# Inverse norms of q and k from Ln and Exp in place of Sqrt and a reciprocal

## The chip, the core and the metric

The kernel runs on one core of a Trainium2 chip. The metric is the time of one execution on the device in microseconds (us), as the median of three runs. TensorE does the matmuls and transposes, VectorE and ScalarE work element by element, GpSimd takes part of the element work, and SyncE issues the transfers. The engines run side by side, each through its own list of instructions in order, and wait for each other by semaphores.

## The reference

The input is 16 sequences (called batches here) of 256 tokens with 128 channels. The kernel computes a small attention block with a modulated layer norm once for each batch, and then a transformer of six layers. Cut to what the change touches, one layer is

```python
def l2norm(t):
    return t / jnp.maximum(jnp.linalg.norm(t, axis=-1, keepdims=True), 1e-12)

def attn_layer(x, Wqkv, qs, ksc, Wo):            # x: batches x 256 x 128, 16 heads of 64
    q, k, v = heads(x @ Wqkv)
    q = l2norm(q) * qs                           # norms over the 64 channels of a head
    k = l2norm(k) * ksc
    q = q * cos * scale + rotate_half(q) * sin * scale
    k = k * cos * inv + rotate_half(k) * sin * inv
    out = local_attention(q, k, v)               # windows of 32 queries, 64 keys, factor 8 ahead of the softmax
    return out @ Wo

for i in range(6):
    x = attn_layer(shift_tokens(x), ...) + x
    x = ffn_layer(shift_tokens(x), ...) + x      # layer norm, gate through gelu, 341 inner channels
```

## The kernel before

After a first block that handles the small attention for all batches, the program walks through 6 layers of 16 batches, 96 batches in all. For each batch every engine goes through a list of short step names that is written out by hand at the top of the file (`PE_ORDER` for TensorE, `DVE_ORDER` for VectorE, `ACT_ORDER` for ScalarE, `POOL_ORDER` for GpSimd, `SP_ORDER` for SyncE). A step listed in `AHEAD` works for the next batch, a step in `BEHIND` for the batch before, and all others for the batch itself. So projections and norms of batch g+1, attention of batch g, and the feed-forward part of batch g-1 run in the same pass. Fourteen of a layer's sixteen batches stand in a loop over layers, unrolled.

The steps that matter here, with their lines:

- XS shifts the tokens. PA, PB (TensorE, L1059) project q and k into two banks of PSUM that are used in turn. RA, RB (VectorE, L829) multiply a projection with the rotary tables into `prod_a` and `prod_b`; AD (GpSimd, L532) adds the two into `ks` (AD0, AD1) or `qs` (AD2, AD3). QA, QB (ScalarE, L614) square a projection.
- NK, NQ (TensorE, L1070) sum the squares of a head, CK, CQ (VectorE, L855) bound the sums from below, TK, TQ (TensorE, L1078) transpose them: now a token is a partition, and 2 x 16 numbers lie beside each other.
- RTK, RTQ (ScalarE, L625) take the square root into `norms`, and IK, IQ (VectorE, L863 and L858) the reciprocal, into `rk` for k and `rq` for q. q is not scaled itself: `rq` enters as the scale of the softmax's exponential and through `neg_max`.
- RK (GpSimd, L502 to L510) splits `rk` into three bfloat16 parts, in four small instructions. TU (TensorE, L1086) transposes them, UC (VectorE, L838) copies them out as `rkt`, KN0 and KN1 (TensorE, L1095) spread them over the channels, and KM (VectorE, L845) multiplies `ks` with that. MK (SyncE) then moves `ks` to `kt`, where the scores read it.
- S (TensorE, L1115 and L1125) writes the scores of half a batch (S00 and S01 the first half, S10 and S11 the second). M0 and M1 (VectorE) take the maxima of these halves (L868) and multiply them with `rq` into `neg_max` (L873). E (ScalarE, L652) takes the exponentials in four parts for each half. T and TC (L1136 and L880) transpose the probabilities and copy them out, PV (L1160) multiplies with v, AT (L890) divides, O and OC (L1144 and L640) transpose again and copy out `att_t`.
- V (TensorE, L1106) projects v; VC (L618 on ScalarE, L849 on VectorE) copies it out.
- LN (ScalarE, L665 and L669) computes the layer norm's factor as Ln and then Exp with a scale of -0.5. G (ScalarE, L676) is the gelu.

ScalarE holds one set of function tables at a time, and a step that needs another set has a load ahead of it in `ACT_ORDER`: LE loads the set that has both Exp and Ln (L634), LS the set of Sqrt (L630), LG the set of Gelu (L632). One batch has LE twice, LS twice and LG once. The first block has loads of its own, which are not changed.

GpSimd's list for a batch is only `AD0 AD1 RK AD2 AD3`, in this order.

Of the kernel before, what the change touches and what calls it, by code (L numbers as in the profile page):

```python
# [10 lines left out]
ACT = mybir.ActivationFunctionType  # L11
AX_X = mybir.AxisListType.X

P = 128
BATCH, TOKENS, DIM = 16, 256, 128
DEPTH, HEADS, DIM_HEAD, WINDOW = 6, 16, 64, 32
INNER = HEADS * DIM_HEAD
DIM_INNER = int(DIM * 4 * 2 / 3)
QK_SCALE = 8.0
PAIRS = HEADS // 2  # L20
TILES = TOKENS // P
# [18 lines left out]
SQRT_SET = "sqrt_and_others"  # L40
# [8 lines left out]
PV01 T10 V3 NQ V4 V5 T11 TQ PV10 O00 PV11 V6 O01 V7 O10 O11  # L49
"""  # L50
DVE_ORDER = """
XS RA0 RB0 M0 RA1 RB1 XA VC1 XB RA2 CK RB2 XG IK M1 TC00 UC H0 H1 KM0 TC01 H2 KM1 RA3 X RB3 AT0 VC3 TC10 CQ TC11
VC5 AT1 IQ VC7
"""
ACT_ORDER = """
QA0 QB0 VC0 LE E00 QB1 QA1 E01 E02 SQ E03 LN LS RTK QB2 QA2 LG G0 G1 VC2 G2 LE E10 E11 QA3 QB3 E12 E13 VC4 LS
RTQ OC00 OC01 VC6 OC10 OC11
"""
POOL_ORDER = """
# [7 lines left out]
def steps_of(text):  # L67

    steps = []
    for word in text.split():  # L70
# [5 lines left out]
PE_ORDER, DVE_ORDER, ACT_ORDER, POOL_ORDER, SP_ORDER = (  # L76
    steps_of(text) for text in (PE_ORDER, DVE_ORDER, ACT_ORDER, POOL_ORDER, SP_ORDER))
AHEAD = ("XS", "V", "VC", "PA", "PB", "RA", "RB", "QA", "QB", "AD", "NK", "NQ", "CK", "CQ", "TK", "TQ", "RTK", "RTQ",
         "IK", "IQ", "RK", "TU", "UC", "KN", "KM", "LW", "MK", "MQ", "LS")
BEHIND = ("WO", "XA", "XB", "CEN", "SQ", "VAR", "LN", "XG", "UP", "G", "H", "DN", "X", "LF", "LG")  # L80


# [5 lines left out]
def rank(order, s, *kinds):  # L88

    return [x for x in order if x[0] in kinds].index(s)  # L90
# [6 lines left out]
def build(nc, t):  # L97

    with ExitStack() as ctx:
        def sb(name, shape, dt=F32):  # L100
            return ctx.enter_context(nc.sbuf_tensor(name, shape, dt))

        def sem(name):
            return ctx.enter_context(nc.semaphore(name))
# [22 lines left out]
        ln_eps, zero_col = (biases[:, i:i + 1] for i in range(2))  # L127
# [22 lines left out]
        ks = sb("ks", [P, 2, QUADS, TOKENS])  # L150
        qs = sb("qs", [P, 2, QUADS, TOKENS])
        norm2 = sb("norm2", [P, TOKENS])
        norms_ = sb("norms", [P, 2, TILES, HEADS])
        rk = sb("rk", [P, TILES, HEADS])
        rk_rest = sb("rk_rest", [P, TILES, HEADS])
        rk_bf = sb("rk_bf", [P, TILES, 3, HEADS], BF16)
# [4 lines left out]
        rq = [sb(f"rq{i}", [P, TILES, HEADS]) for i in range(2)]  # L161
# [32 lines left out]
        def carve(parts, *shape):  # L194
# [9 lines left out]
            if len(shape) == 3:  # L204
# [66 lines left out]
        xs_ready, proj_ready, prod_ready, sq_ready, rot_ready, v_made, v_even_ready, v_odd_ready = (  # L271
            sem(n) for n in ("xs_ready", "proj_ready", "prod_ready", "sq_ready", "rot_ready", "v_made",
                             "v_even_ready", "v_odd_ready"))
        norm_made, clamped, norm_turned, norms_ready, r_ready, rk_parts, rk_turned, rkt_ready, kn_made, kn_ready = (
            sem(n) for n in ("norm_made", "clamped", "norm_turned", "norms_ready", "r_ready", "rk_parts", "rk_turned",
                             "rkt_ready", "kn_made", "kn_ready"))
        k_moved, q_moved, b1_turned = (sem(n) for n in ("k_moved", "q_moved", "b1_turned"))

# [13 lines left out]
        def at(g, per_batch, n=0):  # L292

            return g * per_batch + (CREDIT + n)

        def start_with_credit(eng, *sems):
            for s in sems:
                eng.sem_inc(s, CREDIT)
# [176 lines left out]
        def _(pool):  # L475
# [19 lines left out]
            def step(s, g, b, parity, layer):  # L495
                kind = s[0]
                if kind == "RK":

                    pool.wait_ge(r_ready, at(g, 2, rank(DVE_ORDER, ("IK",), "IK", "IQ") + 1))
                    pool.wait_ge(rk_turned, at(g, 1))  # L500
                    alone(pool)
                    pool.tensor_copy(rk_bf[:, :, 0, :], rk[:, :, :]).then_inc(rk_parts, 1)  # L502
                    pool.wait_ge(rk_parts, at(g, 4, 1))
                    pool.tensor_tensor(rk_rest[:, :, :], rk[:, :, :], rk_bf[:, :, 0, :], ALU.subtract
                                       ).then_inc(rk_parts, 1)
                    pool.wait_ge(rk_parts, at(g, 4, 2))
                    alone(pool)
                    pool.tensor_copy(rk_bf[:, :, 1, :], rk_rest[:, :, :]).then_inc(rk_parts, 1)
                    pool.wait_ge(rk_parts, at(g, 4, 3))
                    pool.tensor_tensor(rk_bf[:, :, 2, :], rk_rest[:, :, :], rk_bf[:, :, 1, :], ALU.subtract  # L510
                                       ).then_inc(rk_parts, 1)
# [25 lines left out]

        @block.scalar
        def _(act):
            start_with_credit(act, sq_ready, norms_ready, v_even_ready, o_copied, exp_ready, xcsq_ready, log_ready, rstd_ready,  # L540
                              gelu_ready, l_x0, l_sq, l_log, l_rstd, p_sq, p_nsq, p_norm, p_qcopied, p_vtok, p_vt2,
                              *e_out, *out_landed)
            act.wait_ge(consts_landed, 16 * n_consts)
# [63 lines left out]
            def step(s, g, b, parity, layer):  # L607
# [12 lines left out]
                if kind in ("RTK", "RTQ"):  # L620

                    n = int(kind == "RTQ")
                    act.wait_ge(norm_turned, at(g, 2, n + 1))
                    act.wait_ge(r_ready, at(g, 2, n))
                    nc.scalar.activation(norms_[:, n, :, :].rearrange("p t (u r) -> p t u r", r=4),  # L625
                                         norm2_t_ps.rearrange("p (t u m) -> p t u m", t=TILES, u=QUADS)[:, :, :, 0:4],
                                         ACT.Sqrt, bias=zero_col[:, :], scale=QK_SCALE ** -2 if n else 1.0
                                         ).then_inc(norms_ready, 1)
                if kind == "LS":
                    nc.scalar.preload_act_table_set(SQRT_SET)  # L630
                if kind == "LG":
                    nc.scalar.preload_act_table_set(GELU_SET)  # L632
                if kind in ("LE", "LF"):
# [53 lines left out]

        @block.vector
        def _(dve):
            start_with_credit(dve, r_ready, v_odd_ready, p_r, xs_ready, prod_ready, clamped, rkt_ready, kn_ready,  # L690
                              max_ready, nb_ready, inv_ready, t_copied, att_ready, x1_ready, xs1_ready, xg_ready,
                              hidden_ready, x_ready, l_mod, l_xc, l_xn, l_h, p_mean, p_inv, p_n, p_n2,
                              p_qfin, p_kv, p_branch, p_x1, *e_fin, *e_mod)
# [24 lines left out]
            n = 4  # L718
# [90 lines left out]
            def step(s, g, b, parity, layer):  # L809
# [40 lines left out]
                if kind in ("CK", "CQ"):  # L850
# [2 lines left out]
                    dve.wait_ge(norm_made, at(g, 2, n + 1))  # L853
                    dve.wait_ge(norm_turned, at(g, 2, n))
                    V.tensor_scalar(norm2[:, :], norm2_ps, NORM_EPS2, None, ALU.max).then_inc(clamped, 1)  # L855
                if kind == "IQ":
                    dve.wait_ge(norms_ready, at(g, 2, 2))
                    V.reciprocal(rq[parity][:, :, :], norms_[:, 1, :, :]).then_inc(r_ready, 1)  # L858
                if kind == "IK":

                    dve.wait_ge(norms_ready, at(g, 2, 1))
                    dve.wait_ge(rk_parts, at(g, 4))
                    V.reciprocal(rk[:, :, :], norms_[:, 0, :, :]).then_inc(r_ready, 1)  # L863
                if kind == "M":
                    i = s[1]
                    dve.wait_ge(s_ready, at(g, TILES, i + 1))
                    for e in range(2):
                        last = V.tensor_reduce(row_max[:, :, e],  # L868
                                               score_ps[e][:, :].rearrange("p (j c) -> p j c", c=KEYS), AX_X, ALU.max)
                    last.then_inc(max_ready, 1)  # L870
                    dve.wait_ge(max_ready, at(g, TILES, i + 1))
                    dve.wait_ge(r_ready, at(g, 2, 2))
                    V.scalar_tensor_tensor(out=neg_max[:, :], in0=row_max[:, :, :].rearrange("p j e -> p (j e)"),  # L873
                                           scalar=-1.0, in1=rq[parity][:, i, :], op0=ALU.mult, op1=ALU.mult
                                           ).then_inc(nb_ready, 1)
# [406 lines left out]
```

## Time and profile before

| what | value |
|---|---|
| three runs | 4441.12, 4441.35, 4457.95 us |
| median | 4441.35 us |
| the profiled execution | 4456.55 us |
| its span, first to last instruction | 4454.8 us |
| TensorE busy | 4076.7 us, 92% |
| ScalarE busy | 3219.2 us, 72% |
| VectorE busy | 2972.1 us, 67% |
| GpSimd busy | 1035.9 us, 23% |

The profile names the engines PE (TensorE's matmuls), PEld (its weight loads), DVE (VectorE), ACT (ScalarE), POOL (GpSimd) and SP (SyncE), and its times come from one execution. Busy shares are means over the whole span. The question to a row is always what ended the wait ahead of it, and who waited for it.

### The profile page before, as it was taken

To read this page: it belongs to the slowest core of one execution; us is meant where nothing else is said; L and a number is where in the kernel's file an instruction comes from. 1 tells how busy PE (TensorE), PEld (TensorE's weight loads), DVE (VectorE), ACT (ScalarE), POOL (GpSimd) and SP (SyncE) were. 2 spreads that over 40 slices of the span, in tenths; PEclk is the share of its full clock that TensorE was granted. 3 is DMA by queue.
4 is the path that set the end of the run, shared out by engine and by line. 5 is a ranking of instruction groups with operands and counts; after the bars stand their busy time and mean duration, and the time that the engine had idled before them with its cause. 6 is when DMAs were issued, how large, how long until landed. Compare 5 with 4: busy or idle time off the path is not lost.

```text
span 4454.8 us, 166735 instructions
## 1 busy us (share of the span) xinstructions
PE 4076.7 (92%) x67065; PEld 2569.6 (58%) x67065; DVE 2972.1 (67%) x5758; ACT 3219.2 (72%) x9361; POOL 1035.9 (23%) x857
## 2 busy tenths in 40 slices
PE   6777999998999998999999999999899999999997
PEld 3333666665666665665665556665556565566655
DVE  3335777776767776777776667776677676677674
ACT  3444877776777876777777778777677777777775
POOL 0002222222222222222222222222222223222220
PEclk9557999999999999999999999999999999999998
DMA  0001222213122222222122222122221222222221
GB/s 21 6 19 48 51 49 59 54 45 78 47 58 59 52 48 74 49 59 59 40 59 66 58 59 53 46 59 64 60 59 43 57 59 54 68 52 48 59 59 40
DMA packets 251159, 233.60 MB, mean 52 GB/s; under 512 B 34264, under 2 KB 247784, under 8 KB 249624
## 3 DMA queue, kind: packets, MB, share of 16 engines
q1 hardware_dynamic: 250392, 222.83, 20.6%
q8 instruction: 548, 8.98, 0.9%
q14 instruction: 219, 1.79, 0.1%
HBM read 19.30 MB, written 2.10 MB: 5 GB/s over the span
## 4 chain that ended last, share of the span: by engine, by line
PE 81%; issue 4%; ACT 3%; SPq 1%; DVE 1%; DMA 1%; POOL 1%; DVEq 0%; ACTq 0%; POOLq 0%
PE ring_ps L1106 16%; PE ring_ps L1059 16%; PE out_ps L1172 7%; PE score_ps L1125 6%; PE out_ps L1160 6%; PE out_ps L1200 6%; PE turn_ps L1144 5%; PE turn_ps L1136 5%; PE small_ps L1070 4%; PE turn_ps L1207 2%; PE score_ps L1115 2%; SPq L420 1%; PE out_ps L1190 1%; PE ring_ps L1095 1%; ACT att_t L640 1%
## 5 line engine op out<-in xcount | busy, mean ns | idle before, releaser
L652 ACT ACTIVATE probs<-score_ps,neg_max,rq 128x64 f32<-128x64 f32 x3072 | 1211.0, 431 | 3.9 <-DVE neg_max L873 1.5
L1106 PE MATMUL ring_ps<-wv,xs 128*64 128x512 f32 x3072 | 828.3, 621 | 37.1 <-ACT square L614 24.3
L1059 PE MATMUL ring_ps<-xs,wqk 128*128 128x256 f32 x3072 | 810.7, 398 | 32.4 <-DVE xs L816 23.7
L532 POOL TENSOR_TENSOR ks<-prod_a,prod_b 128x1024 f32<-128x1024 f32 x192 | 452.1, 2355 | 1617.5 <-DVE prod_b L829 1617.5
L1059 PEld LDWEIGHTS ring_ps<-xs,wqk 128*128 128x128 f32 x3072 | 564.7, 194 | 285.2 <-issue 142.1
L614 ACT ACTIVATE square<-ring_ps,biases 128x512 f32<-128x512 f32 x768 | 499.4, 694 | 315.4 <-DVE prod_a L829 246.7
L652 ACT ACTIVATION_READ_ACCUMULATOR probs<-score_ps,neg_max,rq 128x1 f32 x3072 | 707.8, 230 | 0.0
L829 DVE TENSOR_TENSOR prod_a<-ring_ps,tables 128x512 f32<-128x512 f32 x768 | 492.7, 682 | 213.9 <-PE ring_ps L1059 169.1
L532 POOL TENSOR_TENSOR qs<-prod_a,prod_b 128x1024 f32<-128x1024 f32 x192 | 453.4, 2361 | 606.0 <-DVE prod_b L829 605.8
L829 DVE TENSOR_TENSOR prod_b<-ring_ps,tables 128x512 f32<-128x512 f32 x768 | 491.2, 681 | 92.6 <-PE ring_ps L1059 92.1
L640 ACT ACTIVATE att_t<-turn_ps 128x512 f32<-128x512 f32 x384 | 229.6, 598 | 414.2 <-PE turn_ps L1144 414.2
L1160 PE MATMUL out_ps<-v,pt 64*32 64x64 f32 x24576 | 328.8, 225 | 69.4 <-issue 69.2
L880 DVE COPY pt<-turn_ps 128x512 f32<-128x512 f32 x384 | 263.1, 685 | 182.0 <-PE turn_ps L1136 182.0
L849 DVE COPY v<-ring_ps 128x512 f32<-128x512 f32 x384 | 264.6, 689 | 176.9 <-PE ring_ps L1106 176.8
L890 DVE TENSOR_TENSOR att<-out_ps,inv_sums 128x512 f32<-128x512 f32 x384 | 247.5, 687 | 187.4 <-PE out_ps L1160 184.6
L1160 PEld LDWEIGHTS out_ps<-v,pt 64*32 64x32 f32 x24576 | 273.6, 105 | 142.7 <-issue 142.4
L1172 PE MATMUL out_ps<-att_t,wo 128*128 128x256 f32 x1536 | 349.1, 380 | 0.7 <-ACT att_t L640 0.7
L618 ACT ACTIVATE v<-ring_ps 128x512 f32<-128x512 f32 x384 | 234.4, 610 | 134.2 <-PE ring_ps L1106 131.4
L1125 PEld LDWEIGHTS score_ps<-kt,qt 64*32 64x32 f32 x24576 | 258.7, 105 | 113.7 <-issue 113.2
L1125 PE MATMUL score_ps<-kt,qt 64*32 64x64 f32 x24576 | 297.7, 226 | 22.4 <-issue 21.9
L1172 PEld LDWEIGHTS out_ps<-att_t,wo 128*128 128x128 f32 x1536 | 292.9, 191 | 41.1 <-ACT att_t L640 0.9
L1144 PE MATMUL turn_ps<-ident,att 128*128 128x128 f32 x1536 | 254.4, 288 | 67.7 <-ACT att_t L640 66.7
(156 smaller groups left out, 5454.5 us busy)
## 6 DMA issues: line engine op xcount, KB each, us to landing
kt<-ks SPq DMA_DIRECT2D x768, 128.0 KB
qt<-qs SPq DMA_DIRECT2D x768, 128.0 KB
wqk<-in_L_ffn_Wqkv SPq DMA_DIRECT2D x6, 1024.0 KB, 5.2
wv<-in_L_ffn_Wqkv SPq DMA_DIRECT2D x6, 512.0 KB, 4.9
wo<-in_L_ffn_Wo SPq DMA_DIRECT2D x6, 512.0 KB
v<-in_L_attn_x SPq DMA_DIRECT2D x16, 128.0 KB, 2.1
w<-in_L_ffn_W SPq DMA_DIRECT2D x6, 341.0 KB
out_dram<-qs SPq DMA_DIRECT2D x4, 256.0 KB, 2.2
```

The costliest lines, as they stand in the source:

```text
L532: pool.tensor_tensor(dst, prod_a[p % 2][:, :, :], prod_b[p % 2][:, :, :], ALU.add).then_inc(rot_ready, 1)
L614: nc.scalar.activation(square[p % COUPLES][a][:, :], bank_of(("PB" if a else "PA", p), parity)[:, :], ACT.Square, bias=zero_col[:, :]).the ...
L640: nc.scalar.activation(att_t[:, 4 * c:4 * c + 4, P * i:P * (i + 1)], turn_ps[:, :].rearrange("p (j c) -> p j c", c=P), ACT.Copy).then_inc( ...
L652: last = nc.scalar.activation(probs[i][:, j, e, :], score_ps[e][:, KEYS * j:KEYS * (j + 1)], ACT.Exp, bias=neg_max[:, h:h + 1], scale=rq[p ...
L829: last = V.tensor_tensor((prod_b if a else prod_a)[p % 2][:, f, :] .rearrange("p (u c) -> p u c", u=2), bank[:, :].rearrange("p (u c) -> p ...
L1059: last = mm(bank_of(s, parity)[:, TOKENS * f:TOKENS * (f + 1)], wqk[:, n, 2 * c + f, a, :], xs[:, WINDOW:PADDED], start=True, stop=True)
L1106: last = mm(bank_of(s, parity)[64 * e:64 * e + KEYS, :], xs[:, WINDOW * n:WINDOW * n + KEYS], heads[:, :, e, :], start=True, stop=True)
L1125: last = mm(score_ps[e][WINDOW * w:WINDOW * (w + 1), KEYS * j:KEYS * (j + 1)], qt[64 * e:64 * e + 64, j, q0:q0 + WINDOW], kt[64 * e:64 * e ...
L1144: last = pe.transpose(turn_ps[:, P * j:P * (j + 1)], att[i][:, 4 * c + j, :, :].rearrange("p e k -> p (e k)"), ident[:, :])
L1160: last = mm(out_ps[e][WINDOW * w:WINDOW * (w + 1), DIM_HEAD * j:DIM_HEAD * (j + 1)], pt[64 * e:64 * e + 64, j, WINDOW * w:WINDOW * (w + 1) ...
L1172: last = mm(out_ps[0][:, 0:TOKENS], wo[:, j, :], att_t[:, j, :], start=(j == 0), stop=(j == PAIRS - 1))
L1200: last = mm(out_ps[c % 2][0:size, TOKENS * n:TOKENS * (n + 1)], w1[:, col:col + size], xg[:, :], start=True, stop=True)
```

## The change

RTK and RTQ take Ln of the summed squares into a new tile `log_norm2` and then Exp of -0.5 times that, straight into `rk` or `rq`. That is the inverse norm, so the reciprocals IK and IQ and their tile go. Both functions are in the set that the softmax uses. The two LS loads of a batch go, and the LE ahead of E00, since ScalarE still has that set then; LG and the LE behind the last gelu stay. GpSimd's RK and VectorE's M now wait for `norms_ready`, which Exp raises.

```diff
@@ orders @@
 DVE_ORDER = """
-XS RA0 RB0 M0 RA1 RB1 XA VC1 XB RA2 CK RB2 XG IK M1 TC00 UC H0 H1 KM0 TC01 H2 KM1 RA3 X RB3 AT0 VC3 TC10 CQ TC11
-VC5 AT1 IQ VC7
+XS RA0 RB0 M0 RA1 RB1 XA VC1 XB RA2 CK RB2 XG M1 TC00 UC H0 H1 KM0 TC01 H2 KM1 RA3 X RB3 AT0 VC3 TC10 CQ TC11
+VC5 AT1 VC7
 ACT_ORDER = """
-QA0 QB0 VC0 LE E00 QB1 QA1 E01 E02 SQ E03 LN LS RTK QB2 QA2 LG G0 G1 VC2 G2 LE E10 E11 QA3 QB3 E12 E13 VC4 LS
+QA0 QB0 VC0 E00 QB1 QA1 E01 E02 SQ E03 LN RTK QB2 QA2 LG G0 G1 VC2 G2 LE E10 E11 QA3 QB3 E12 E13 VC4
 RTQ OC00 OC01 VC6 OC10 OC11
@@ GpSimd, RK @@
-                    pool.wait_ge(r_ready, at(g, 2, rank(DVE_ORDER, ("IK",), "IK", "IQ") + 1))
+                    pool.wait_ge(norms_ready, at(g, 2, 1))
@@ ScalarE, RTK and RTQ @@
                     act.wait_ge(norm_turned, at(g, 2, n + 1))
-                    act.wait_ge(r_ready, at(g, 2, n))
-                    nc.scalar.activation(norms_[:, n, :, :].rearrange("p t (u r) -> p t u r", r=4),
+                    if n:
+                        dst = rq[parity][:, :, :]
+                    else:
+                        act.wait_ge(rk_parts, at(g, 4))
+                        dst = rk[:, :, :]
+                    nc.scalar.activation(log_norm2[:, n, :, :].rearrange("p t (u r) -> p t u r", r=4),
                                          norm2_t_ps.rearrange("p (t u m) -> p t u m", t=TILES, u=QUADS)[:, :, :, 0:4],
-                                         ACT.Sqrt, bias=zero_col[:, :], scale=QK_SCALE ** -2 if n else 1.0
+                                         ACT.Ln, bias=zero_col[:, :], scale=QK_SCALE ** -2 if n else 1.0
+                                         ).then_inc(logs_ready, 1)
+                    act.wait_ge(logs_ready, at(g, 2, n + 1))
+                    nc.scalar.activation(dst, log_norm2[:, n, :, :], ACT.Exp, bias=zero_col[:, :], scale=-0.5
                                          ).then_inc(norms_ready, 1)
-                if kind == "LS":
-                    nc.scalar.preload_act_table_set(SQRT_SET)
@@ VectorE, IQ, IK and M @@
-                if kind == "IQ":
-                    dve.wait_ge(norms_ready, at(g, 2, 2))
-                    V.reciprocal(rq[parity][:, :, :], norms_[:, 1, :, :]).then_inc(r_ready, 1)
-                if kind == "IK":
-
-                    dve.wait_ge(norms_ready, at(g, 2, 1))
-                    dve.wait_ge(rk_parts, at(g, 4))
-                    V.reciprocal(rk[:, :, :], norms_[:, 0, :, :]).then_inc(r_ready, 1)
...
-                    dve.wait_ge(r_ready, at(g, 2, 2))
+                    dve.wait_ge(norms_ready, at(g, 2, 2))
```

ScalarE's rows behind the layer norm's factor, before the change (a row is an instruction with its line, output and inputs; `square_1` is QB2):

```order
L665 ACTIVATE log_var<-out_ps,biases 128x256 [waits var_ready]
L669 ACTIVATE rstd<-log_var,biases 128x256 [waits xg_ready,log_ready]
L630 ACT_TABLE_LOAD
L623 REGISTER_ALU
L625 ACTIVATE norms<-small_ps,biases 128x32 [waits r_ready,norm_turned]
L612 REGISTER_ALU
L614 ACTIVATE square_1<-ring_ps,biases 128x512 [waits norm_made,prod_ready]
```

The same place after the change:

```order
L670 ACTIVATE log_var<-out_ps,biases 128x256 [waits var_ready]
L674 ACTIVATE rstd<-log_var,biases 128x256 [waits xg_ready,log_ready]
L623 REGISTER_ALU
L627 ISA [waits norm_turned]
L629 ACTIVATE log_norm<-small_ps,biases 128x32 [waits rk_parts]
L634 ACTIVATE rk<-log_norm,biases 128x32 [waits logs_ready]
L612 REGISTER_ALU
L614 ACTIVATE square_1<-ring_ps,biases 128x512 [waits norm_made,prod_ready]
```

The load has gone from between `rstd` and RTK, and two instructions that both need the set already loaded end with `rk`.

VectorE's rows around M1 before the change, from RB2's second product to the first hidden chunk:

```order
L829 TENSOR_TENSOR prod_b<-ring_ps,tables 128x512
L915 ISA [waits rstd_ready]
L916 SCALAR_TENSOR_TENSOR xg<-out_ps,ln_vecs,rstd 128x256 [waits w1_ready]
L863 RECIPROCAL rk<-norms 128x32 [waits rk_parts,norms_ready]
L868 TENSOR_REDUCE row_max<-score_ps 128x8 [waits s_ready]
L868 TENSOR_REDUCE row_max<-score_ps 128x8
L873 SCALAR_TENSOR_TENSOR neg_max<-row_max,rq 128x16 [waits r_ready,max_ready]
L878 ISA
L879 REGISTER_ALU [waits t_made]
L880 COPY pt<-turn_ps 128x512 [waits pv_ready]
L838 COPY rkt<-ring_ps 48x256 [waits kn_made,rk_turned]
```

The same place after the change:

```order
L834 TENSOR_TENSOR prod_b<-ring_ps,tables 128x512
L912 ISA [waits rstd_ready]
L913 SCALAR_TENSOR_TENSOR xg<-out_ps,ln_vecs,rstd 128x256 [waits w1_ready]
L865 TENSOR_REDUCE row_max<-score_ps 128x8 [waits s_ready]
L865 TENSOR_REDUCE row_max<-score_ps 128x8
L870 SCALAR_TENSOR_TENSOR neg_max<-row_max,rq 128x16 [waits norms_ready,max_ready]
L875 ISA
L876 REGISTER_ALU [waits t_made]
L877 COPY pt<-turn_ps 128x512 [waits pv_ready]
L843 COPY rkt<-ring_ps 48x256 [waits kn_made,rk_turned]
```

M1's two maxima now follow XG directly, and `rk` no longer passes through VectorE. GpSimd's and TensorE's rows are the same as before, apart from the semaphore that RK waits for.

## Rows read from the trace of the kernel before

**Rows 1.** The page: TensorE's line, granted clock in 40 slices, the last chain.

```profile
PE 4076.7 (92%) x67065; PEld 2569.6 (58%) x67065; DVE 2972.1 (67%) x5758; ACT 3219.2 (72%) x9361; POOL 1035.9 (23%) x857
...
PEclk9557999999999999999999999999999999999998
...
PE 81%; issue 4%; ACT 3%; SPq 1%; DVE 1%; DMA 1%; POOL 1%; DVEq 0%; ACTq 0%; POOLq 0%
```

**Rows 2.** TensorE's groups by form: busy us, mean ns | idle before, what ended it.

```profile
L1106 PE MATMUL ring_ps<-wv,xs 128*64 128x512 f32 x3072 | 828.3, 621 | 37.1 <-ACT square L614 24.3 <-issue 12.5
...
L1144 PE MATMUL turn_ps<-ident,att 128*128 128x128 f32 x1536 | 254.4, 288 | 67.7 <-ACT att_t L640 66.7 <-issue 0.9
...
L1095 PE MATMUL ring_ps<-rkt,head_sel_bf 48*128 48x256 bf16 x384 | 75.3, 277 | 9.1 <-DVE rkt L838 8.9 <-issue 0.2
```

**Rows 3.** ScalarE's groups by form, the same columns.

```profile
L630 ACT ACT_TABLE_LOAD x192 | 246.3, 1283 | 3.3
...
L640 ACT ACTIVATE att_t<-turn_ps 128x512 f32<-128x512 f32 x384 | 229.6, 598 | 414.2 <-PE turn_ps L1144 414.2
```

**Rows 4.** Timeline of one batch around E00: start us, us, engine, line.

```profile
2079.00 2.35 POOL L532 TENSOR_TENSOR ks<-prod_a,prod_b 128x1024 f32<-128x1024 f32 x1 [13.40 <-DVE prod_b L829]
2080.29 1.10 DVE L873 SCALAR_TENSOR_TENSOR neg_max<-row_max,rq 128x16 f32<-128x16 f32 x1
2081.06 1.28 ACT L634 ACT_TABLE_LOAD   x1
...
2082.69 1.28 DVE L829 TENSOR_TENSOR prod_b<-ring_ps,tables 128x512 f32<-128x512 f32 x2
...
2084.01 0.69 ACT L614 ACTIVATE square<-ring_ps,biases 128x512 f32<-128x512 f32 x1
```

**Rows 5.** Timeline of the same batch, from the layer norm's factor to KN0.

```profile
2090.74 0.51 ACT L669 ACTIVATE rstd<-log_var,biases 128x256 f32<-128x256 f32 x1
...
2091.27 1.28 ACT L630 ACT_TABLE_LOAD   x1
2091.34 1.48 PE L1125 MATMUL score_ps<-kt,qt 64*32 64x64 f32 x128
...
2092.56 0.29 ACT L625 ACTIVATE norms<-small_ps,biases 128x32 f32<-128x32 f32 x1
2092.75 1.26 ACT L614 ACTIVATE square<-ring_ps,biases 128x512 f32<-128x512 f32 x2
...
2092.88 0.35 DVE L863 RECIPROCAL rk<-norms 128x32 f32<-128x32 f32 x1 [0.40 <-ACT norms L625]
...
2094.41 0.18 DVE L873 SCALAR_TENSOR_TENSOR neg_max<-row_max,rq 128x16 f32<-128x16 f32 x1
...
2094.68 2.36 POOL L532 TENSOR_TENSOR qs<-prod_a,prod_b 128x1024 f32<-128x1024 f32 x1
...
2096.20 0.39 PE L1095 MATMUL ring_ps<-rkt,head_sel_bf 48*128 48x256 bf16 x2
```

**Rows 6.** Timeline of a batch in which the second half's scores are late.

```profile
2010.25 0.66 PE L1125 MATMUL score_ps<-kt,qt 64*32 64x64 f32 x41 [0.67 <-issue]
...
2012.08 2.35 POOL L532 TENSOR_TENSOR qs<-prod_a,prod_b 128x1024 f32<-128x1024 f32 x1
2012.28 2.18 DVE L873 SCALAR_TENSOR_TENSOR neg_max<-row_max,rq 128x16 f32<-128x16 f32 x1
...
2015.40 0.38 PE L1095 MATMUL ring_ps<-rkt,head_sel_bf 48*128 48x256 bf16 x2 [1.04 <-DVE rkt L838]
```

**Rows 7.** Timeline: IK and KN0, first and last of 85 ordinary batches.

```profile
501.52 0.35 DVE L863 RECIPROCAL rk<-norms 128x32 f32<-128x32 f32 x1 [0.59 <-ACT norms L625]
...
504.93 0.39 PE L1095 MATMUL ring_ps<-rkt,head_sel_bf 48*128 48x256 bf16 x2
...
4361.92 0.35 DVE L863 RECIPROCAL rk<-norms 128x32 f32<-128x32 f32 x1 [0.45 <-ACT norms L625]
...
4365.33 0.39 PE L1095 MATMUL ring_ps<-rkt,head_sel_bf 48*128 48x256 bf16 x2
```

More of the change, by code:

```diff
@@ L78 @@
 AHEAD = ("XS", "V", "VC", "PA", "PB", "RA", "RB", "QA", "QB", "AD", "NK", "NQ", "CK", "CQ", "TK", "TQ", "RTK", "RTQ",
-         "IK", "IQ", "RK", "TU", "UC", "KN", "KM", "LW", "MK", "MQ", "LS")
+         "RK", "TU", "UC", "KN", "KM", "LW", "MK", "MQ", "LS")
 BEHIND = ("WO", "XA", "XB", "CEN", "SQ", "VAR", "LN", "XG", "UP", "G", "H", "DN", "X", "LF", "LG")
@@ L152, in build @@
         norm2 = sb("norm2", [P, TOKENS])
-        norms_ = sb("norms", [P, 2, TILES, HEADS])
+        log_norm2 = sb("log_norm2", [P, 2, TILES, HEADS])
         rk = sb("rk", [P, TILES, HEADS])
@@ L273, in build @@
                              "v_even_ready", "v_odd_ready"))
-        norm_made, clamped, norm_turned, norms_ready, r_ready, rk_parts, rk_turned, rkt_ready, kn_made, kn_ready = (
-            sem(n) for n in ("norm_made", "clamped", "norm_turned", "norms_ready", "r_ready", "rk_parts", "rk_turned",
+        norm_made, clamped, norm_turned, norms_ready, logs_ready, rk_parts, rk_turned, rkt_ready, kn_made, kn_ready = (
+            sem(n) for n in ("norm_made", "clamped", "norm_turned", "norms_ready", "logs_ready", "rk_parts", "rk_turned",
                              "rkt_ready", "kn_made", "kn_ready"))
@@ L539, in _ @@
         def _(act):
-            start_with_credit(act, sq_ready, norms_ready, v_even_ready, o_copied, exp_ready, xcsq_ready, log_ready, rstd_ready,
+            start_with_credit(act, sq_ready, logs_ready, norms_ready, v_even_ready, o_copied, exp_ready, xcsq_ready, log_ready, rstd_ready,
                               gelu_ready, l_x0, l_sq, l_log, l_rstd, p_sq, p_nsq, p_norm, p_qcopied, p_vtok, p_vt2,
@@ L689, in _ @@
         def _(dve):
-            start_with_credit(dve, r_ready, v_odd_ready, p_r, xs_ready, prod_ready, clamped, rkt_ready, kn_ready,
+            start_with_credit(dve, v_odd_ready, p_r, xs_ready, prod_ready, clamped, rkt_ready, kn_ready,
                               max_ready, nb_ready, inv_ready, t_copied, att_ready, x1_ready, xs1_ready, xg_ready,
```

## The prediction

> **What bounds the kernel now.** I read the page first. TensorE is busy 92% of the span, and the chain that ended last runs 81% through TensorE and only 3% through ScalarE [rows 1]. So a ScalarE instruction is worth something only where TensorE waits for it, and I went next to TensorE's own waits, in the list of groups with the idle time ahead of each [rows 2]. The largest that names another engine has nothing to do with the norms: 67.7 us at the transposes of `att`, which wait for the copy of their own single bank. Two are near the change. V matmuls wait 24.3 us for a ScalarE square, and KN0 (L1095, which spreads the inverse norms of k) waits 8.9 us for `rkt`. Last I laid one ordinary batch out in time [rows 4, 5], one in which TensorE reached its scores late [rows 6], and the same instructions of all batches [rows 7].
>
> **What is removed from ScalarE.** Per batch go two loads of the square-root set, L630, 192 in all at 1283 ns, and one of the two L634 loads, also 1.28 us [rows 4], so 3 x 1.28 = 3.85 us [rows 3]. Two Sqrt of 0.29 us [rows 5] become two Ln, and two Exp are new. No trace row has Ln or Exp at 128x32; the nearest is Sqrt on the same tile, and I take 0.29 us for each. ScalarE is relieved of 3.85 - 0.58 = 3.27 us a batch, 314 us in 96 batches. I cost that at nothing, place by place:
> - The load before E00 (LE). The load ends at 2082.34, and M0's `neg_max` ends at 2081.39, so E00 could start 0.9 us earlier. But behind E00 stands QB1, which starts at 2084.01, right after VectorE's `prod_b` ends at 2083.97 [rows 4]. VectorE is not changed there, so QB1 and all behind it start as before. The 0.9 us becomes idle time.
> - The load before RTQ. Its consumers are `rq`, which is read a batch later, and the OC copies to `att_t`, which stand behind it on ScalarE and spend 414 us in the run waiting for TensorE's transposes [rows 3]: ScalarE has time to spare there.
> - The load before RTK. This one has a consumer close behind, and it is where the change acts.
>
> What covers the first two is TensorE's 92%. If that cover were gone (the V waits of 24.3 us), it would be the first rival below. VectorE's two reciprocals go as well: IK 0.35 us [rows 5], and IQ, which stands ahead of one copy only and is taken as nothing between zero and the same 0.35 us, since no wait of TensorE names that copy.
>
> **What is late next.** Follow RTK in [rows 5]. `rstd` ends at 2091.25, the load takes 2091.27 to 2092.55, Sqrt ends at 2092.85, IK runs 2092.88 to 2093.23, GpSimd then splits `rk` (RK), and 1.45 us after IK's end its large addition AD2 starts, 2094.68 to 2097.04. Without the load, Ln starts where the load did, Exp follows it at the 0.03 us by which IK follows Sqrt, and `rk` is there at 2091.27 + 0.29 + 0.03 + 0.29 = 2091.88. QB2 starts 0.10 us ahead of Sqrt's end (2092.75 against 2092.85), so Ln may start as much ahead of `rstd`'s end: 2091.76. I take the middle, 2091.82, or 1.41 us earlier than 2093.23. RK and AD2 move with it: AD2 runs 2093.27 to 2095.63. Its operands from RB2 do not hold it: RB2 is ahead of IK in VectorE's order, and VectorE had been idle for 0.40 us when IK started, so RB2 was done before 2092.5.
>
> Now `neg_max` of M1. Before, IK holds M1 back and holds RK back as well, and `neg_max` starts at 2094.41, 0.27 us ahead of AD2, and takes 0.18 us. [rows 6] show the other order: the scores end at 2010.91, `neg_max` starts 1.37 us later, at 2012.28, when AD2 is already running (2012.08 to 2014.43), takes 2.18 us instead of 0.18, and ends 0.03 us after AD2. [rows 4] show it for M0: `neg_max` from 2080.29 ends at 2081.39, AD0 at 2081.35. So while GpSimd's addition runs, this VectorE instruction doesn't finish. After the change the scores of [rows 5] still end at 2092.82, `neg_max` can start at 2092.82 + 1.37 = 2094.19, and AD2 has been running since 2093.27. The race that was won by 0.27 us is lost by 0.9 us, in every batch.
>
> The Trainium skill (SBUF — State Buffer, section "Who interferes with whom") gives the rule: a VectorE instruction with two inputs in SBUF and a GpSimd instruction that reads SBUF exclude each other, and whichever issues second blocks fully until the first is done. `neg_max` reads `row_max` and `rq`, both in SBUF. By that rule the 2.18 us is no accident of one batch, and the trace agrees; it is a rule that speaks against this change, because the change alters who issues first.
>
> **The price.** In [rows 6] KN0 starts 0.97 us after AD2's end (2015.40 against 2014.43): through `neg_max`, the copy TC00, the copy UC to `rkt`, and the semaphore (the 0.97 us hold all of it). So KN0 of [rows 5] can't start before 2095.63 + 0.97 = 2096.60; it started at 2096.20, and TensorE would wait 0.40 us. Measured from the start of IK before the change, the new time is 3.72 us. The old distance is 3.41 us in the first and the last of the 85 ordinary batches [rows 7], 3.32 us in [rows 5], and 3.36 us in the mean of the 85. The stall is 3.72 - 3.36 = 0.36 us a batch, 85 x 0.36 = 31 us. Nothing behind makes it up: H0, KM0, TC01, H2 and KM1 queue on VectorE behind UC and move by about the same, and TensorE has no other work ahead of KN0.
>
> In the ten batches with late scores the change helps: there AD2 ends 1.41 us earlier, `neg_max` is let go earlier, and the waits for `rkt`, 8.9 us over the run [rows 2], are gone or nearly so. Sum: +31 - 9 = +22 us. The first batch, where TensorE waits for QA1 behind the load, gives back up to the 0.9 us of [rows 4]. Sum +21 us.
>
> The profiled execution took 4456.55 us (span 4454.8 us); the sum gives it 4478. The median of the three runs is 4441.35 us, 15 us below; carried over, **4462 us**, 0.5% slower. What a measurement of this kernel can tell from no change is 0.5%, 22 us.
>
> Bounds. If Ln and Exp were free beyond the fixed part of the nearest row (AD2 0.1 us earlier than taken), the stall is 0.26 us a batch, net +12 us. If Ln and Exp take as much as the 0.51 us of `rstd` each [rows 5], KN0 comes at 3.72 + 0.44 = 4.16 us and the stall is 0.80 us a batch, 68 - 10 = +58 us. I keep near the first, since Sqrt on the same tile is 0.29 us.
>
> **The rivals.**
> - Faster: ScalarE's relief reaches the V matmuls. The 24.3 us that they wait for squares [rows 2] go, and the 8.9 us at KN0, and `neg_max` costs nothing: 4441 - 33 = 4408 us. It needs QA and QB to be late for ScalarE's own queue. Against it: at 2084.01 the square follows VectorE's product by 0.04 us [rows 4], so ScalarE was waiting, not late. It decides from about two thirds of the 24.3 us on. Chance 0.04.
> - No stall: AD2 doesn't block `neg_max` as in [rows 6], or RK starts later than I think, because GpSimd is slow to see ScalarE's semaphore, and `neg_max` wins again. Then only the 9 to 10 us are left, 4431 us. To win, AD2 would have to start 0.9 us later than worked out, which is two thirds of the 1.41 us gained. Chance 0.10.
> - The stall costs clock as well. The granted clock is near full, 2.4 GHz, in the slices of the steady part and at five to seven tenths where the first part with its gaps is, with stretches at 1.2 GHz [rows 1], so new gaps could add such stretches. The `att` wait, 67.7 us in 96 batches or 0.7 us in each [rows 2], is longer than the new gap, and the slices still show nine tenths or more, which speaks against it. If each fourth batch lost 1 us more, 24 us: 4486 us. Chance 0.08.
> - The Trainium skill (ScalarE: Activation LUTs, section "What ACT_TABLE_LOAD costs") says that a switch costs about 2.66 us, of which 1.38 us is a drain. The trace disagrees: Sqrt starts 0.01 us after the load's end [rows 5]. With that price `rk` would come up to 1.4 us earlier again, AD2 would be over when `neg_max` wants to start, and the time would be the 4431 us of the second rival; 0.01 of that rival's chance is for it.
>
> **How the numbers follow.** Forecast 0.76: stall of 0.25 to 0.55 us a batch, 4452 to 4480 us, slightly more of it above 4463.6 (0.5%) than a third, 0.37, and 0.39 below. The no-stall case (0.10) lies within 0.5%, the clock case (0.08) above it, the first rival (0.04) below, and 0.02 is for the unforeseen on the slow side. Slower 0.37 + 0.08 + 0.02 = 0.47; within 0.5% 0.39 + 0.10 = 0.49; faster 0.04. The range from 4430 to 4484 us holds the no-stall case and leaves out the fast rival, the upper half of the clock case and the upper end of the bounds, under 0.2 together.
>
> **What would show it.** Right: M1's `neg_max` at about 1.5 us in nearly all batches, ending with AD2; a wait of KN0 for `rkt` of some 0.4 us in each of 80 and more batches; QB1 still right behind `prod_b`; ScalarE's busy share down by about 7 points. Wrong: `neg_max` at 0.18 us, KN0 without waits, or a wait of similar size that has gone to another instruction. The prediction fails most easily on the distance of two events 0.4 us apart: 0.1 us in Ln or Exp is 8 us in the sum.

## The result and the profile after

The changed kernel takes 4461.72 us (median of 18 runs, 4455.78 to 4470.33), beside 4441.74 us (18 runs, 4431.88 to 4457.95) for the kernel before, taken together with it. The ratio is 1.0042, with a 95% interval of 1.0032 to 1.0051: some 20 us slower, a little under the 0.5% that can be told from no change without many runs. The forecast was 4462 us. The profiled execution took 4467.11 us (span 4465.3 us), and its mean granted clock was 0.960 of full speed, against 0.959 before.

First the page of the changed kernel: busy times, granted clock in 40 slices, and the chain that ended last.

```profile
PE 4064.6 (91%) x66873; PEld 2568.1 (58%) x67065; DVE 2995.3 (67%) x5566; ACT 2910.5 (65%) x9265; POOL 1035.6 (23%) x857
...
PEclk9557999999999999999999999999999999999998
...
PE 75%; issue 8%; ACT 3%; DVE 3%; SPq 1%; POOL 1%; DMA 1%; DVEq 0%; POOLq 0%; ACTq 0%
```

ScalarE is busy 308.7 us less than in [rows 1], and the kernel is no faster for it. VectorE has lost its two reciprocals and is busier all the same (2995.3 against 2972.1 us). The granted clock of the slices is the same. In the chain TensorE's share fell from 81% to 75%, and VectorE's rose from 1% to 3%. (TensorE's busy time can't be compared: 192 matmul records are missing from this trace, half of the masks' at L1112. The k part below has all its records and the same shares of the chain.)

Where VectorE's time went, and who waits for it, is in the groups by form (busy us, mean ns | idle before, what ended it).

```profile
L1103 PE MATMUL ring_ps<-wv,xs 128*64 128x512 f32 x3072 | 830.3, 622 | 37.0 <-ACT square L614 24.4 <-issue 12.5
...
L870 DVE SCALAR_TENSOR_TENSOR neg_max<-row_max,rq 128x16 f32<-128x16 f32 x192 | 213.3, 1111 | 7.1
...
L1092 PE MATMUL ring_ps<-rkt,head_sel_bf 48*128 48x256 bf16 x384 | 74.6, 272 | 25.4 <-DVE rkt L843 24.2 <-issue 0.2
...
L645 ACT ACTIVATE att_t<-turn_ps 128x512 f32<-128x512 f32 x384 | 229.3, 597 | 424.5 <-PE turn_ps L1141 424.5
```

KN0 waits 24.2 us for `rkt` instead of 8.9, the V matmuls wait for squares as long as before (24.4 against 24.3 us), both [rows 2], and the copies to `att_t` wait 10 us longer for TensorE than in [rows 3]. `neg_max` takes 1111 ns in the mean; before it was 645 ns (123.9 us in 192).

The timeline shows the same batch as [rows 4, 5], first around E00, then from the layer norm's factor to KN0.

```profile
2079.30 2.35 POOL L532 TENSOR_TENSOR ks<-prod_a,prod_b 128x1024 f32<-128x1024 f32 x1 [13.37 <-DVE prod_b L834]
2080.59 1.09 DVE L870 SCALAR_TENSOR_TENSOR neg_max<-row_max,rq 128x16 f32<-128x16 f32 x1
2081.72 0.41 ACT L657 ACTIVATE probs<-score_ps,neg_max,rq 128x64 f32<-128x64 f32 x1 [0.40 <-DVE neg_max L870]
...
2084.29 1.27 ACT L614 ACTIVATE square<-ring_ps,biases 128x512 f32<-128x512 f32 x2 [0.92 <-DVE prod_b L834]
...
2091.01 0.51 ACT L674 ACTIVATE rstd<-log_var,biases 128x256 f32<-128x256 f32 x1
2091.42 0.27 ACT L629 ACTIVATE log_norm<-small_ps,biases 128x32 f32<-128x32 f32 x1
2091.72 0.33 ACT L634 ACTIVATE rk<-log_norm,biases 128x32 f32<-128x32 f32 x1
...
2093.49 2.35 POOL L532 TENSOR_TENSOR qs<-prod_a,prod_b 128x1024 f32<-128x1024 f32 x1
...
2094.47 1.40 DVE L870 SCALAR_TENSOR_TENSOR neg_max<-row_max,rq 128x16 f32<-128x16 f32 x1
2095.80 0.68 DVE L877 COPY pt<-turn_ps 128x512 f32<-128x512 f32 x1
2096.40 0.27 DVE L843 COPY rkt<-ring_ps 48x256 bf16<-48x256 bf16 x1
...
2096.81 0.38 PE L1092 MATMUL ring_ps<-rkt,head_sel_bf 48*128 48x256 bf16 x2 [0.26 <-DVE rkt L843]
```

Around E00, what the load had taken is now idle time: the square starts 0.92 us after ScalarE is free, when VectorE's `prod_b` is done. Further down, `rk` is there 0.53 us after `rstd`'s end (2092.05 against 2091.52); in [rows 5] it was 1.98 us. AD2 starts 1.44 us behind `rk`, `neg_max` is issued 0.98 us behind AD2's start, takes 1.40 us where it took 0.18, ends 0.03 us after AD2, and KN0 waits. In 90 of the 96 batches M1's `neg_max` is now longer than 0.5 us; before it was 10.

A batch with late scores (the one of [rows 6]) in the timeline after:

```profile
2011.95 2.35 POOL L532 TENSOR_TENSOR qs<-prod_a,prod_b 128x1024 f32<-128x1024 f32 x1
...
2013.34 0.99 DVE L870 SCALAR_TENSOR_TENSOR neg_max<-row_max,rq 128x16 f32<-128x16 f32 x1
2014.86 0.27 DVE L843 COPY rkt<-ring_ps 48x256 bf16<-48x256 bf16 x1
...
2015.36 0.39 PE L1092 MATMUL ring_ps<-rkt,head_sel_bf 48*128 48x256 bf16 x2
```

Here the earlier AD2 helps: `neg_max` takes 0.99 us instead of 2.18, and KN0 has no wait where it had 1.04 us.

The list of waits begins at the modelled end of the V matmul ahead of KN0, and a KN0 that waits for nothing starts 0.07 us before that end. I also took from the rows of all batches behind the first how much later than this KN0 starts. The sum is 9.9 us before and 30.7 us after. After, batches whose scores end more than 2.4 us behind the transposes TK (1.84 us is usual; there are 12) have none of it, and the other 83 have 30.7 us, 0.37 us each in the mean.

### The profile page after: what moved, and what is told of

Read it like the earlier page. It is cut to its first block, busy times and chain, and to the rows that moved or that the text cites. A ratio compares the mean times of both kernels' runs of the same rounds, so it can differ in the third digit from the quotient of the medians.

```text
span 4465.3 us, 165988 instructions
## 1 busy us (share of the span) xinstructions
PE 4064.6 (91%) x66873; PEld 2568.1 (58%) x67065; DVE 2995.3 (67%) x5566; ACT 2910.5 (65%) x9265; POOL 1035.6 (23%) x857
## 4 chain that ended last, share of the span: by engine, by line
PE 75%; issue 8%; ACT 3%; DVE 3%; SPq 1%; POOL 1%; DMA 1%; DVEq 0%; POOLq 0%; ACTq 0%
PE ring_ps L1056 16%; PE ring_ps L1103 15%; PE out_ps L1169 7%; PE out_ps L1157 6%; PE score_ps L1122 6%; PE turn_ps L1141 5%; PE small_ps L1067 4%; PE turn_ps L1133 4%; PE out_ps L1197 3%; PE turn_ps L1204 2%; PE score_ps L1112 2%; SPq L420 1%; PE out_ps L1187 1%; PE ring_ps L1092 1%; ACT att_t L645 1%
## 5 line engine op out<-in xcount | busy, mean ns | idle before, releaser
L1103 PE MATMUL ring_ps<-wv,xs 128*64 128x512 f32 x3072 | 830.3, 622 | 37.0 <-ACT square L614 24.4
L1056 PE MATMUL ring_ps<-xs,wqk 128*128 128x256 f32 x3072 | 811.6, 398 | 34.3 <-DVE xs L821 24.2
L657 ACT ACTIVATION_READ_ACCUMULATOR probs<-score_ps,neg_max,rq 128x1 f32 x3072 | 698.6, 227 | 0.0
```

Of the source, the lines that this page charges most:

```text
L657: last = nc.scalar.activation(probs[i][:, j, e, :], score_ps[e][:, KEYS * j:KEYS * (j + 1)], ACT.Exp, bias=neg_max[:, h:h + 1], scale=rq[p ...
L1056: last = mm(bank_of(s, parity)[:, TOKENS * f:TOKENS * (f + 1)], wqk[:, n, 2 * c + f, a, :], xs[:, WINDOW:PADDED], start=True, stop=True)
L1103: last = mm(bank_of(s, parity)[64 * e:64 * e + KEYS, :], xs[:, WINDOW * n:WINDOW * n + KEYS], heads[:, :, e, :], start=True, stop=True)
```

## The experiments

The theory that the prediction rests on: the 20 us are the price of a lost race at M1 (GpSimd's AD2 is issued ahead of VectorE's `neg_max`, which then doesn't finish until AD2 has), and the time taken off ScalarE is worth nothing. The rivals: the time is lost elsewhere (Ln and Exp, clock, other gaps), or ScalarE's relief does reach TensorE and hides a larger loss. All ratios are against the kernel before, whose median was 4442.96 us (34 runs) beside the first four kernels and 4440.41 us (27 runs) beside the other four. The columns behind the ratio are from the groups by form of each kernel's profile: the mean of all 192 `neg_max`, and the idle time ahead of KN's matmuls.

| kernel | median us | ratio, 95% | `neg_max`, ns | idle ahead of KN, us |
|---|---|---|---|---|
| before | see above | 1 | 645 | 9.1 |
| changed | 4461.72 | 1.0042 (1.0032 to 1.0051) | 1111 | 25.4 |
| AD2 behind M1 | 4425.31 | 0.9967 (0.9953 to 0.9982) | 556 | 1.0 |
| one more load | 4451.65 | 1.0021 (1.0007 to 1.0035) | 679 | 13.4 |
| q part only | 4447.18 | 1.0013 (1.0000 to 1.0026) | 719 | 16.6 |
| k part only | 4455.52 | 1.0028 (1.0014 to 1.0043) | 1149 | 28.4 |
| before, AD2 behind M1 | 4423.77 | 0.9964 (0.9951 to 0.9977) | 558 | 0.3 |
| `row_max` in PSUM | 4426.29 | 0.9969 (0.9955 to 0.9982) | 175 | 1.0 |
| AD2 in halves | 4427.03 | 0.9970 (0.9958 to 0.9981) | 727 | 2.4 |
| both AD behind M | 4421.25 | 0.9960 (0.9946 to 0.9974) | 175 | 0.8 |

**AD2 behind M1's neg_max, in the changed kernel.** The order of the two is forced by a wait on GpSimd, at AD2 alone.

```diff
+                    if p == 2 and not (isinstance(g, int) and g == 0):
+                        pool.wait_ge(nb_ready, at(g, TILES))
```

> The changed kernel, with GpSimd's AD2 made to wait until M1's neg_max is done; nothing else differs. Lost race (my theory): the 20 us come from AD2 that is issued 0.9 us ahead of neg_max, so with the order forced KN0's waits for rkt (22 us in the window 420:4455 of the changed kernel) fall under 5 us, the mean of neg_max falls from 1111 ns to about 650 (M0's are still held by AD0), and the time falls from 4461.7 to 4437 to 4446 us. Rival 1, the time is lost elsewhere (Ln and Exp themselves, gaps at other matmuls, the clock): the waits for rkt may go, but the time stays at 4455 us or more. Rival 2, AD2 that is later by up to 1.4 us makes the move of q late: slower than 4462 us, with a new wait of TensorE's scores.

It took 4425.31 us, lower than expected, and lower than both kernels. The timeline of the same batch:

```profile
2069.28 0.32 ACT L636 ACTIVATE rk<-log_norm,biases 128x32 f32<-128x32 f32 x1
...
2072.02 0.17 DVE L872 SCALAR_TENSOR_TENSOR neg_max<-row_max,rq 128x16 f32<-128x16 f32 x1
2072.28 2.36 POOL L534 TENSOR_TENSOR qs<-prod_a,prod_b 128x1024 f32<-128x1024 f32 x1 [1.19 <-DVE neg_max L872]
2073.28 0.28 DVE L845 COPY rkt<-ring_ps 48x256 bf16<-48x256 bf16 x1 [0.40 <-PE ring_ps L1085]
...
2074.04 0.39 PE L1094 MATMUL ring_ps<-rkt,head_sel_bf 48*128 48x256 bf16 x2
```

`neg_max` takes 0.17 us, AD2 waits 1.19 us for it, and now VectorE's copy to `rkt` is the one that waits, 0.40 us for TensorE's transposes. The idle time ahead of KN fell from 25.4 to 1.0 us. Nothing else was changed, so the loss of the change is this race: forcing the order takes away all of it and more. Rival 1 falls: Ln, Exp and the clock are the same in this kernel. Rival 2 falls too, AD2 that starts later made nothing late. The time is 18 us under the kernel before beside it (15 us by the ratio), and the theory as I had it gave 9 at most; the next experiments bear on that.

**One table load more, ahead of RTK.** The list of ScalarE gets a load where the load of the square root had stood.

```diff
-QA0 QB0 VC0 E00 QB1 QA1 E01 E02 SQ E03 LN RTK QB2 QA2 LG G0 G1 VC2 G2 LE E10 E11 QA3 QB3 E12 E13 VC4
+QA0 QB0 VC0 E00 QB1 QA1 E01 E02 SQ E03 LN LS RTK QB2 QA2 LG G0 G1 VC2 G2 LE E10 E11 QA3 QB3 E12 E13 VC4
...
+                if kind == "LS":
+                    nc.scalar.preload_act_table_set(LN_EXP_SET)
```

> The changed kernel, with one table load of 1.28 us more, ahead of RTK, where the square-root load had stood: three loads a batch, 123 us more of ScalarE time than in the changed kernel. Lost race: rk is ready 1.28 us later, AD2 starts near 2.2 + 1.28 = 3.5 us after the transposes TK instead of 2.2 us, neg_max (which wants to start at 3.2 us) wins again and takes 0.18 us at M1, and the kernel is faster for a longer ScalarE: 4434 to 4446 us. Rival 1 (Ln and Exp or the clock cost the time): 4455 to 4465 us. Rival 2 (ScalarE's relief is worth something to TensorE, and what is lost is more than that): slower than the changed kernel, 4470 us or more.

A load that computes nothing makes the changed kernel faster, 4451.65 instead of 4461.72 us, and the intervals of the two ratios hardly overlap. The timeline:

```profile
2082.82 0.51 ACT L676 ACTIVATE rstd<-log_var,biases 128x256 f32<-128x256 f32 x1
2083.35 1.28 ACT L637 ACT_TABLE_LOAD   x1
...
2084.65 0.29 ACT L629 ACTIVATE log_norm<-small_ps,biases 128x32 f32<-128x32 f32 x1
...
2084.97 0.32 ACT L634 ACTIVATE rk<-log_norm,biases 128x32 f32<-128x32 f32 x1
...
2086.29 0.19 DVE L872 SCALAR_TENSOR_TENSOR neg_max<-row_max,rq 128x16 f32<-128x16 f32 x1
...
2086.73 2.36 POOL L532 TENSOR_TENSOR qs<-prod_a,prod_b 128x1024 f32<-128x1024 f32 x1
```

`neg_max` is ahead of AD2 by 0.44 us and takes 0.19 us. In the run it loses in 13 batches, where it lost in 10 before and 90 in the changed kernel. The direction is the theory's; the size isn't: 4434 to 4446 us were expected. 4 us of the excess are in the rows (idle time of 13.4 us ahead of KN against 9.1), the other 5 I can't place, and they lie within the interval of the ratio (6 us to either side).

**The two parts alone.** For q, RTQ by Ln and Exp, and RTK with its load, Sqrt and IK; for k the reverse. The core of the edit for q (for k the condition is `n == 0`; the lists get LS and IK, or LE, LS and IQ, back at their old places):

```diff
+                    if n == 1:
...
+                        nc.scalar.activation(log_norm2[:, n, :, :].rearrange("p t (u r) -> p t u r", r=4), turned,
+                                             ACT.Ln, bias=zero_col[:, :], scale=scale).then_inc(logs_ready, 1)
+                        act.wait_ge(logs_ready, at(g, 1, 1))
+                        nc.scalar.activation(dst, log_norm2[:, n, :, :], ACT.Exp, bias=zero_col[:, :], scale=-0.5
+                                             ).then_inc(norms_ready, 1)
+                    else:
+                        act.wait_ge(r_ready, at(g, 1))
+                        nc.scalar.activation(norms_[:, n, :, :].rearrange("p t (u r) -> p t u r", r=4), turned,
+                                             ACT.Sqrt, bias=zero_col[:, :], scale=scale).then_inc(norms_ready, 1)
...
+                if kind == "IK":
...
+                    V.reciprocal(rk[:, :, :], norms_[:, 0, :, :]).then_inc(r_ready, 1)
```

> Only the inverse norms of q by Ln and Exp (no table load ahead of RTQ and none ahead of E00, no IQ); those of k by load, Sqrt and reciprocal as before. Lost race: this part was costed at nothing, so 4436 to 4446 us, like the kernel before at 4441.7, with M1's neg_max at 0.18 us in the ordinary batches. Rival 2 (ScalarE's relief of two loads a batch, 246 us in all, reaches TensorE): under 4430 us. Rival 3 (the q part carries the loss, through later or earlier E00 and rq): 4455 us or more.

> Only the inverse norms of k by Ln and Exp (no load and no IK around RTK); those of q by load, Sqrt and reciprocal, with the load ahead of E00 as before. Lost race: all of the loss is here, 4455 to 4470 us, with KN0's waits for rkt near 22 us and M1's neg_max at 1.4 us and more. Rival 3 (the q part carries the loss): 4436 to 4446 us.

The groups of TensorE by form, of the q part and then of the k part:

```profile
L1107 PE MATMUL ring_ps<-rkt,head_sel_bf 48*128 48x256 bf16 x384 | 75.2, 276 | 16.6 <-DVE rkt L853 16.4 <-issue 0.2
```

```profile
L1105 PE MATMUL ring_ps<-rkt,head_sel_bf 48*128 48x256 bf16 x384 | 74.6, 272 | 28.4 <-DVE rkt L853 27.2 <-issue 0.2
```

The q part takes two loads a batch, 246 us, off ScalarE, and is not faster: 4447.18 us, a ratio of 1.0013 whose interval begins at 1. Rival 2, under 4430 us, falls. The k part has the lost race (M1's `neg_max` over 0.5 us in 90 batches) and most of the loss. Rival 3, which put the loss into the q part (4455 us or more there, 4436 to 4446 us for the k part), falls too. The q part's median lies 1 us above what I had expected, and the k part's inside it, half a microsecond from its lower edge. The two excesses, 0.13% and 0.28%, make the 0.42% of the whole change, but each interval is 0.13% or more to either side, so that sum is weak evidence. In the q part M1 lost the race in 17 batches instead of 10, though the steps between `rstd` and M1 are those of the kernel before. All but one of the 17 have scores that end more than 2.4 us behind TK. Such late batches number 14 in the profiled execution before, 16 in that of the q part, and from 5 to 16 over the ten profiled executions; whether the q part's surplus is chance or its doing stays open.

**The kernel before, with AD2 behind M1.** The same two lines as in the first experiment, in the kernel before.

> The kernel before, with AD2 made to wait until M1's neg_max is done. Lost race: there only the ten or so batches with late scores have the lost race, so what there is to win is their wait for rkt, 8.9 us in the run: 4430 to 4440 us, waits for rkt under 3 us. Rival 1 (the order of AD2 and neg_max costs TensorE nothing): 4441.7 us, no difference that can be told.

It took 4423.77 us. Its group of KN:

```profile
L1097 PE MATMUL ring_ps<-rkt,head_sel_bf 48*128 48x256 bf16 x384 | 75.0, 276 | 0.3 <-issue 0.2
```

That is below the 4430 to 4440 us expected: the race cost the kernel before about 16 us (0.36%, 0.23 to 0.49%), not 9. With the first experiment this makes a square of four kernels: with the race open, 4441.7 us before and 4461.7 after; with the order forced, 4423.8 and 4425.3. Each was taken beside its own runs of the kernel before, so the ratios are what to compare. Where the race can't be lost, three loads, two Sqrt and two reciprocals a batch against two Ln and two Exp make no difference that can be told: ratios of 0.9964 and 0.9967, each with an interval of 0.13% (6 us) or a little more to either side. Within that, it is the direct measure of what ScalarE's 309 us are worth here.

**row_max in PSUM.** In the changed kernel AD2 stays as early as it is, but one input of `neg_max` moves out of SBUF, into space that the norms' sums leave free at that time. The added waits only guard that space.

```diff
-        row_max = sb("row_max", [P, PAIRS, 2])
+        row_max = small_ps[:, 0:HEADS].rearrange("p (j e) -> p j e", e=2)
...
+                    if i and not (isinstance(g, int) and g == DEPTH * BATCH - 1):
+                        dve.wait_ge(norms_ready, at(g, 2, 3))
...
+                    if not (isinstance(g, int) and g == 0):
+                        pe.wait_ge(nb_ready, at(g, TILES, n - 1))
```

> The changed kernel, with row_max kept in PSUM (in the space of the norms' sums, with the waits that this needs) instead of SBUF, so that neg_max reads one tile in SBUF and one in PSUM; AD2 is issued as early as in the changed kernel. If it is the two inputs from SBUF that are blocked while GpSimd adds: neg_max takes 0.2 to 0.35 us though AD2 runs, at M0 and at M1, its sum falls from 213 us to under 60, the waits for rkt nearly go, and the time is 4430 to 4446 us, in spite of AD2 not having moved. Rival 1 (the time is lost elsewhere): 4455 to 4465 us. Rival 4 (any VectorE instruction that reads SBUF is held while GpSimd adds): neg_max stays at 1.1 us in the mean, 4455 to 4465 us.

The timeline of the batch, and the view of the tile `neg_max` (ns: least, median, most):

```profile
2074.39 2.35 POOL L532 TENSOR_TENSOR qs<-prod_a,prod_b 128x1024 f32<-128x1024 f32 x1
...
2075.48 0.17 DVE L874 SCALAR_TENSOR_TENSOR neg_max<-small_ps,rq 128x16 f32<-128x16 f32 x1
...
2077.40 0.39 PE L1098 MATMUL ring_ps<-rkt,head_sel_bf 48*128 48x256 bf16 x2
```

```profile
L874 DVE SCALAR_TENSOR_TENSOR neg_max<-small_ps,rq x192: 173/175/176, 397.0 to 4357.7; 128x16 f32<-128x16 f32 x192
```

`neg_max` starts 1.09 us into AD2 and takes 0.17 us; in none of 192 cases does it take more than 176 ns. Issue order is that of the changed kernel (M1's `neg_max` starts while AD2 runs in 93 of 96 batches, there in 94), so what blocks is where the inputs lie. Rival 4 falls, since `neg_max` still reads `rq` from SBUF. The Trainium skill (SBUF — State Buffer, section "Who interferes with whom") says that a VectorE instruction with at most one input in SBUF, outside its two-port performance modes, does not contend with GpSimd; this run agrees, with 173 to 176 ns in all 192 cases. The gain is that of the forced order, 4426.29 us.

**AD2 in halves.** Two additions of 512 columns each in the changed kernel.

```diff
+                    if p == 2:
+                        for a in range(2):
+                            last = pool.tensor_tensor(dst[:, a], prod_a[p % 2][:, a, :], prod_b[p % 2][:, a, :], ALU.add)
+                        last.then_inc(rot_ready, 1)
```

> The changed kernel, with AD2 issued as two additions of half the size, about 1.2 us each. If neg_max is held until the GpSimd instruction that was issued ahead of it is done: it gets in between the halves, some 1.1 us earlier than before, so it takes 0.2 to 0.8 us at M1 and the time is 4434 to 4446 us. Rival 5 (GpSimd keeps the memory as long as it has work): neg_max still ends with the second half, and the time stays at 4455 to 4466 us.

The timeline (the two halves are one row, of 1.27 us each in the mean):

```profile
2072.71 2.50 POOL L534 TENSOR_TENSOR qs<-prod_a,prod_b 128x512 f32<-128x512 f32 x2
...
2073.64 0.38 DVE L875 SCALAR_TENSOR_TENSOR neg_max<-row_max,rq 128x16 f32<-128x16 f32 x1
...
2075.66 0.39 PE L1097 MATMUL ring_ps<-rkt,head_sel_bf 48*128 48x256 bf16 x2
```

`neg_max` ends at 2074.02; the first half, at 1.27 us, ends at 2073.98, and the second follows it without a pause. The other batches agree: in 71 of 96, M1's `neg_max` starts 0.04 us or more ahead of the first half's end and ends 0.03 to 0.09 us behind it; in 23 it starts later and ends 0.03 us behind the second half; in two it starts behind both. So it is held for the one GpSimd instruction that was issued ahead of it, and gets in between two. Rival 5 falls. The time is 4427.03 us.

**Both additions behind their neg_max.** The edit of the first experiment, and AD0 behind M0.

```diff
+                    if p == 0 and not (isinstance(g, int) and g == 0):
+                        pool.wait_ge(nb_ready, at(g, TILES, -1))
```

> The changed kernel, with AD2 made to wait for M1's neg_max, and AD0 for M0's. Lost race: neg_max takes 0.18 us everywhere, sum under 45 us; at M1 this gives what the first experiment gives, 4437 to 4446 us. At M0 the blocked neg_max delays E00, which the prediction found hidden behind prod_b, so nothing more is won: within 5 us of the first experiment. Rival 2 (E00 earlier by 0.9 us does reach TensorE): 10 us or more below the first experiment. Rival 6 (AD0 that is later makes the move of k late): slower than the first experiment.

`neg_max` is now 175 ns in the mean, and the time is 4421.25 us, 4 us below the first experiment and within both intervals. M0's blocked `neg_max`, 1.1 us in most batches, costs nothing that can be measured, since E00 behind it is hidden. It is the fastest version here, 0.4% under the kernel before, but the five versions in which KN0 no longer pays for the race can't be told apart. All five came in below the times expected of them, by 4 to 16 us.

## Why the prediction was right

- **ScalarE's relief costed at nothing.** Right at each place: around E00 0.92 us of new idle time ahead of QB1, 0.9 forecast; the V waits unchanged; the `att_t` copies wait longer. The square of four kernels shows it for the sum.
- **rk earlier, AD2 with it.** Forecast 1.41 us; 1.45 us in the rows, counted from `rstd`'s end. Ln takes 0.27 and Exp 0.33 us where 0.29 us each was taken. The load's price is that of its row: in the experiment with one more load, Ln starts 0.02 us after the load's end, and `rk` comes 1.43 us later than without. The rival by the 2.66 us of the Trainium skill (ScalarE: Activation LUTs, section "What ACT_TABLE_LOAD costs") has no support in these runs.
- **The lost race.** Forecast 0.9 us late in every batch; measured 0.98 us in the batch shown, and the race is lost in 90 of 96 batches, not in every one.
- **The stall.** KN0 0.97 us after AD2's end, forecast and measured. 0.36 us a batch forecast, 0.37 us measured in the mean of 83 batches (78 of them have a stall over 0.05 us), 31 us in all both ways.
- **What late batches give back.** Forecast 8.9 us; their waits are gone, and the sum over all batches went from 9.9 to 30.7 us, a net +20.8 beside the +22 of the sum and the +20 of the medians. Between the first and the last KN0, though, the two profiled executions differ by 8.6 us only: the one before, 15 us above its median, lost some 12 us elsewhere that I have not placed. The up to 0.9 us of the first batch can't be seen: the first KN0 of the two profiled executions lie 2.5 us apart, and that of the first experiment 4 us from the changed kernel's.
- **The rivals.** No stall: the 4431 us that it gave are near what the kernel takes once `neg_max` can't be blocked (4421 to 4427 us). Clock: 0.960 against 0.959.

What the prediction undervalued is the race in the kernel before. It took that as 8.9 us, the waits listed at KN0; without it, 16 us go. Of those 9.4 us are the shift of KN0 (9.9 to 0.5 us in the forced version). The rest, and some 3 us of the 33 between the changed kernel and its forced version (0.75% less 29.8 us at KN0), I have not placed; the intervals are as wide. One way is that the 8.9 us came from one execution with 10 lost races. The q part and the kernel with one more load, where `rk` comes about as late as before, show 17 and 13 of them, and shifts of KN0 of 17.8 and 14.1 us. That this holds for the kernel before is not shown. So 21 us against 20 is closer than the terms deserve: the mechanism and the stall of a batch were right, what the race cost before was put at 8.9 us where it is about 16, and that the difference still came out to a microsecond is partly luck.

## What to carry to other kernels

Work taken off an engine that TensorE does not wait for was worth nothing here, and what it releases earlier can take something else's place: ask of each event that moves which instruction it now overtakes. Where GpSimd works on SBUF beside VectorE, look for short VectorE instructions with two SBUF inputs whose duration in the profile varies tenfold (0.17 to 2.29 us in the kernel before); make them come first by a wait, put one input in PSUM, or cut GpSimd's instruction, and do that before tuning anything else around them. Here each of the three brought the kernel to 4425 to 4427 us.

## What the runs showed of the hardware

That a blocked instruction of VectorE gets in between two back-to-back instructions of GpSimd (0.38 us in the batch shown, though the second half follows the first at once) I had expected only as one of two ways. The other surprise is how sharp the condition is: the same instruction, in the same place beside the same addition, took 1.40 us with both inputs in SBUF and 0.17 us with one in PSUM.
